# The feed-forward part behind the attention loop: batches taken by strip, products ahead in four banks, eight output buffers

## The reference, cut to what matters

```python
x = x + attn(cond(x, ...))
# low rank, ids choose A[i] (512 x 16) and B[i] (16 x 512) for each batch
y = (x @ B[i].T) @ A[i].T
# feed-forward part
h = layernorm(y) * gamma + beta
h = fake_quant(h) @ fake_quant(w1).T + b1      # a scale for each row: max|h| / 127
h = gelu(h)
h = fake_quant(h) @ fake_quant(w3).T + b3
out = x + h
```

## Time and profile before

| | |
|---|---|
| median of 3 runs | 602.52 us (602.12 to 605.37) |
| the profiled execution, its own time | 599.33 us |
| its span, first to last instruction | 597.5 us |
| busy over the span: PE, DVE, POOL, ACT | 95%, 83%, 67%, 55% |
| mean granted clock of PE | 0.99 of full |

### The profile page before, as it was taken

One profiled execution on the slowest core, in us unless ns is written; L12 is line 12 of the kernel. 1 busy time (PEld: TensorE's weight loads), 2 busy tenths in 40 slices (PEclk: granted clock), 3 DMA queues, 4 the chain that ended last, 5 costly groups with the idle time before them and its releaser, 6 DMA issues. The chain is left out here.

```text
span 597.5 us, 10369 instructions
## 1 busy us (share of the span) xinstructions
PE 568.8 (95%) x3107; PEld 430.4 (72%) x3107; DVE 495.5 (83%) x643; ACT 327.4 (55%) x877; POOL 401.0 (67%) x410
## 2 busy tenths in 40 slices
PE   6999979999999999999999999999999999987985
PEld 4545658888887788888878887888878888773342
DVE  2974558998999799979997999799979998867696
ACT  2142456556554655565556555655565555557594
POOL 3004288698679867976897689769966997751053
PEclk9999999999999999999999999999999999999699
DMA  9931334512451245124412442254123422100003
GB/s 277 250 70 35 82 95 125 128 49 57 133 127 47 58 128 132 42 60 135 123 45 60 131 114 53 55 146 103 51 66 107 105 47 59 36 1 0 1 2 142
DMA packets 38173, 51.93 MB, mean 87 GB/s; under 512 B 12101, under 2 KB 20453, under 8 KB 38149
## 3 DMA queue, kind: packets, MB, share of 16 engines
q1 hardware_dynamic: 35076, 45.89, 29.6%
q10 hardware_dynamic: 2592, 4.53, 2.3%
q0 software_dynamic: 480, 1.22, 0.6%
HBM read 28.55 MB, written 2.10 MB: 51 GB/s over the span
## 5 line engine op out<-in xcount | busy, mean ns | idle before, releaser
L1015 DVE SCALAR_TENSOR_TENSOR accT<-pair,so_now,accT 128x1024 f32<-128x1024 f32 x125 | 157.6, 1278 | 20.6 <-PE pair L1284 19.8
L1001 DVE SCALAR_TENSOR_TENSOR raw_q<-pair,sc_now,raw_q 128x1024 f32<-128x1024 f32 x90 | 115.5, 1283 | 3.5
L1283 PE MATMUL pair<-ctx_hi,wo 128*128 128x512 f32 x256 | 104.9, 410 | 2.6 <-issue 1.5
L677 ACT ACTIVATE probs<-flow,negmax 128x128 f32<-128x128 f32 x248 | 87.3, 369 | 34.3 <-DVE negmax L966 34.3
L1283 PE MATMUL pair<-h_hi,wq 128*128 128x512 f32 x240 | 100.9, 420 | 1.8 <-ACT raw_q L720 1.7
L1284 PE MATMUL pair<-ctx_lo,wo 128*128 128x512 f32 x256 | 100.4, 392 | 0.0
L1284 PE MATMUL pair<-h_lo,wq 128*128 128x512 f32 x240 | 94.4, 393 | 0.0
L528 POOL TENSOR_TENSOR probs<-probs,rowinv 128x512 f32<-128x512 f32 x64 | 66.7, 1042 | 28.3 <-DVE rowinv L988 28.3
L509 POOL TENSOR_TENSOR qT<-rope_c,rope_s 128x512 f32<-128x512 f32 x62 | 79.4, 1280 | 4.4
L497 POOL TENSOR_TENSOR rope_s<-swap_q,consts 128x512 f32<-128x512 f32 x62 | 80.3, 1295 | 2.1 <-DMA swap_q<-raw_q 2.1
L497 POOL TENSOR_TENSOR rope_c<-raw_q,consts 128x512 f32<-128x512 f32 x62 | 78.5, 1286 | 0.6
(11 more groups left out here) (229 smaller groups left out, 989.3 us busy)
## 6 DMA issues: line engine op xcount, KB each, us to landing
swap_q<-raw_q SPq DMA_DIRECT2D x62, 256.0 KB, 3.5
wq_i<-in_L_attn_qw_q SPq DMA_DIRECT2D x8, 1024.0 KB, 6.0
wo_i<-in_L_attn_qw_o SPq DMA_DIRECT2D x32, 256.0 KB, 2.7
swap_k<-raw_k SPq DMA_DIRECT2D x14, 256.0 KB, 3.6
wkv_i<-in_L_attn_qw_k SPq DMA_DIRECT2D x8, 256.0 KB, 3.8
wkv_i<-in_L_attn_qw_v SPq DMA_DIRECT2D x8, 256.0 KB, 4.0
out<-probsT SPq DMA_DIRECT2D x8, 256.0 KB, 2.0
stage<-in_x ACTq DMA_DIRECT2D x4, 256.0 KB, 4.6
```

The lines of the kernel that those rows point to most:

```text
L677: e = act.activation(probs[:, 0, f, seq(b)], bank[:, seq(b)], ACT.Exp, bias=negmax[:, f, b:b + 1], accum_out=rowsum[:, f, b:b + 1])
L1001: dve.scalar_tensor_tensor(out=into, in0=flat(pair[pair_of(h, (kind, j), last)][:, :, :]), scalar=sc_now[:, scale_slot(kind, h), j:j + 1], ...
L1015: dve.scalar_tensor_tensor(out=a, in0=flat(pair[pair_of(h, (O, c), last)][:, :, :]), scalar=so_now[:, (h if c == 0 else h - 1) % 2, c:c + ...
L1283: pe.matmul(into[:, f, :], w, upper[:, half[f]], start=True, stop=False)
```

## The change

1. The feed-forward part takes the batches in `LOW_ORDER`. "Batch b" there is now the b-th in this order; the number `LOW_ORDER[b]` is used where `low_h`, `rstd`, `accT` and `out` are addressed.
2. Four scaled products go out ahead, each as soon as the statistics of its bank are taken, in four banks (0, 2, 4, 6), one strip each. The other four go in two pairs of different strips (`scaled_pair`), a pair waiting once for `ln_done`.
3. The first two residuals are turned into banks 3 and 7, freed by ACT's squares, and bank 4 takes the others from the third on. The turned rows of the second layer use bank 3, those of its last batch bank 1.
4. Each of the eight batches has its own output buffer. The waits for landed DMAs go away.
5. The hand-written orders of PE, ACT, DVE and POOL are laid out anew. A few waits on buffers that the old order implied are now written out (`gelu_done` ahead of `scale_product(0, b)`, `ln_done` and `res_kept` ahead of the second layer's first products).

The numbers of each operation stay the same.

```diff
+        y_out = [t[:, f, :] for t in (probsT, swap_q, swap_k, probs[:, 1, :, :]) for f in range(2)]
...
-        SCALED, RESID = [banks[0], banks[2]], banks[4]
+        SCALED = [banks[0], banks[2], banks[4], banks[6], banks[0], banks[2], banks[0], banks[2]]
+        RESID = [banks[3], banks[7]] + [banks[4]] * (B - 2)
...
-                sp.dma_start(out[b, :, :], y_out[:, b % 2, :]).then_inc(d_out[b % 2], 16)
+                sp.dma_start(out[LOW_ORDER[b], :, :], y_out[b]).then_inc(d_out[b % 2], 16)
...
-                dve.scalar_tensor_tensor(out=y_ln[b], in0=SCALED[b % 2], scalar=rstd[:, 0, b:b + 1], in1=rows[:, 1, :],
+                dve.scalar_tensor_tensor(out=y_ln[b], in0=SCALED[b], scalar=rstd[:, 0, LOW_ORDER[b]:LOW_ORDER[b] + 1], in1=rows[:, 1, :],
...
+                if not m and b >= 2:
+                    dve.wait_ge(gelu_done, b - 1)
...
-                dve.wait_ge(d_out[b % 2], 16 * (b // 2))
-                dve.tensor_tensor(y_out[:, b % 2, :], probs[:, 0, b % 2, :], resid[b], ALU.add).then_inc(out_late, 1)
+                dve.tensor_tensor(y_out[b], probs[:, 0, b % 2, :], resid[b], ALU.add).then_inc(out_late, 1)
...
             norm(0)
+            norm(1)
             find_top(0, 0)
-            norm(1)
...
             def scaled_product(b):
-
-                if b == 0:
-                    pe.wait_ge(low_scaled, 1)
-                if b < 2:
-                    pe.wait_ge(stats_done, b + 1)
-                else:
-                    pe.wait_ge(ln_done, b - 1)
-                pe.matmul(SCALED[b % 2], low_h[STRIPS[b // 2], seq(b % 2)], low_gT[STRIPS[b // 2], :], start=True, stop=True).then_inc(scaled_done, 1)
+                seat = LOW_ORDER[b]
+                pe.matmul(SCALED[b], low_h[STRIPS[seat // 2], seq(seat % 2)], low_gT[STRIPS[seat // 2], :], start=True, stop=True).then_inc(scaled_done, 1)
+
+            def scaled_pair(p):
+                pe.wait_ge(ln_done, 4 * p - 6)
+                scaled_product(2 * p)
+                scaled_product(2 * p + 1)
...
-            scaled_product(0)
+            pe.wait_ge(low_scaled, 1)
+            for b in range(HB):
+                pe.wait_ge(stats_done, b + 1)
+                scaled_product(b)
             turn_residual(0)
-            scaled_product(1)
-            scaled_product(2)
             turn_residual(1)
...
```

More of the change, by code:

```diff
@@ L289, in two_seqs, with turned_rows @@
             return slice(2 * q * P, (2 * q + 2) * P)
-        SCALED, RESID = [banks[0], banks[2]], banks[4]
+        SCALED = [banks[0], banks[2], banks[4], banks[6], banks[0], banks[2], banks[0], banks[2]]
+        RESID = [banks[3], banks[7]] + [banks[4]] * (B - 2)
         LATE_OUT = 4
-        def turned_rows(m):
-            return banks[1 + 2 * m][:, 0:C * P // 2].bitcast(F16)
+        def turned_rows(m, b):
+            return banks[3 if m and b < B - 1 else 1][:, 0:C * P // 2].bitcast(F16)
         def layer_bank(m, b):
@@ L585, in _ @@
             add_bias(4)
+            add_residual(0)
             add_bias(5)
-            add_residual(0)
+            add_residual(1)
             add_bias(6)
-            add_residual(1)
             add_bias(7)
@@ L793, in keep_residual @@
                 act.wait_ge(resT_done, b + 1)
-                act.activation(resid[b], RESID, ACT.Copy).then_inc(res_kept, 1)
+                act.activation(resid[b], RESID[b], ACT.Copy).then_inc(res_kept, 1)
             def keep_yT(m, b):
                 act.wait_ge(yT_done[m], b + 1)
-                act.activation(y_qT[:, m, b % 2, :, :], turned_rows(m).rearrange("p (c n) -> p c n", c=C),
+                act.activation(y_qT[:, m, b % 2, :, :], turned_rows(m, b).rearrange("p (c n) -> p c n", c=C),
                                ACT.Copy, bias=-HALF_ZERO).then_inc(yT_kept[m], 1)
@@ L839, in _ @@
             keep_yT(1, 1)
+            round_rows(0, 7)
+            keep_yT(0, 6)
             round_rows(1, 2)
[L841 to L843 removed]
+            keep_yT(0, 7)
             gelu_rows(4)
             round_rows(1, 3)
[L846 removed]
             keep_yT(1, 2)
@@ L1142, in _ @@
             find_top(0, 5)
+            norm(6)
+            scale_product(0, 2)
             find_top(1, 0)
-            scale_product(0, 2)
+            norm(7)
+            scale_product(0, 3)
             find_top(1, 1)
-            norm(6)
-            scale_product(0, 3)
             find_top(0, 6)
-            find_top(1, 2)
-            norm(7)
             scale_product(0, 4)
             find_top(0, 7)
+            scale_product(1, 0)
+            find_top(1, 2)
+            scale_product(0, 5)
             find_top(1, 3)
-            scale_product(0, 5)
-            scale_product(1, 0)
+            scale_product(1, 1)
+            scale_product(0, 6)
             find_top(1, 4)
-            scale_product(0, 6)
-            scale_product(1, 1)
             find_top(1, 5)
             scale_product(0, 7)
-            find_top(1, 6)
             scale_product(1, 2)
             scale_product(1, 3)
+            find_top(1, 6)
             find_top(1, 7)
@@ L1504, in turn_residual @@
                     pe.wait_ge(b3_added, C)
-                    pe.wait_ge(stats_done, 3)
+                if b < 2:
+                    pe.wait_ge(squares_done, 2 * b + 2)
+                elif b == 2:
+                    pe.wait_ge(ln_done, 3)
                 else:
@@ L1508, in turn_residual @@
                 for c in range(C):
-                    mm = pe.transpose(RESID[:, seq(c)], accT[:, c, seq(b)], ident)
+                    mm = pe.transpose(RESID[b][:, seq(c)], accT[:, c, seq(LOW_ORDER[b])], ident)
                 mm.then_inc(resT_done, 1)
@@ L1515, in turn_rows @@
                 pe.wait_ge(rounded[m], b + 1)
-                if b >= 1:
+                if m == 1 and b == B - 1:
+                    pe.wait_ge(yT_kept[0], B)
+                elif b >= 1:
                     pe.wait_ge(yT_kept[m], b)
+                elif m == 1:
+                    pe.wait_ge(res_kept, 1)
                 for c in range(C):
-                    mm = pe.transpose(turned_rows(m)[:, seq(c)], rounded_rows(m, b)[:, seq(c)], ident_h[:, :])
+                    mm = pe.transpose(turned_rows(m, b)[:, seq(c)], rounded_rows(m, b)[:, seq(c)], ident_h[:, :])
                 mm.then_inc(yT_done[m], 1)
@@ L1525, in layer @@
                     pe.wait_ge(ff_scaled[0], b)
+                if m == 1 and b == 0:
+                    pe.wait_ge(ln_done, HB)
+                if m == 1 and b == 1:
+                    pe.wait_ge(res_kept, 2)
                 if m == 1 and b >= 2:
```

72 lines of the change are left out of this document (31 added, 41 removed).

## The result

| | before | with the change |
|---|---|---|
| median, us | 602.32 (4 runs, 600.44 to 605.37) | 594.02 (4 runs, 592.96 to 594.74) |
| ratio, with its 95% interval | | 0.9856 (0.9811 to 0.9901) |
| the profiled execution: time, span | 599.33, 597.5 | 592.96, 591.1 |
| its mean granted clock | 0.990 | 0.993 |
| first `norm` to the end of the last residual | 41.95 | 36.44 |

The kernel is 8.3 us faster. I had forecast 3.7 us, and no more than 5.7 us within the range (602.52 to 596.8). The change was timed a second time on another chip, in six runs against seventeen of before: 594.66 us (593.48 to 596.79) against 601.39 (598.17 to 603.63), ratio 0.990 (0.9869 to 0.9932), so 6.7 us. Both are more than forecast.

The account below looks back on a forecast made before the run. DVE was taken to bound the tail, with PE the bound at the low clock. Terms of 1.6 and 2.5 us made 4.1, taken as 3.7: 602.52 to 598.8 us, range 596.8 to 602.4.

Parts of the forecast that it names:

- The bound: Tail from the first `norm`: DVE carries the most work, idle 8.2 us, the most any order can give.
- The pair, the products ahead, the buffers: Tail: four products ahead cost the path nothing, a low-clock pair takes 2.0 us, eight buffers remove 1.9 us of DMA waits.
- Term two: From `scale_product(0, 1)` to the last residual: DVE waits fall from 3.4 to 0.9 us, 2.5 us gained.
- Term one: From the first `norm` to `scale_product(0, 1)`: that product starts at 565.6 instead of 567.21, 1.6 us earlier.
- I leave the low clock from 554.54 to 564.8: Start of the tail: the half-clock stretch stays where it was, since PE's wait ahead of it stays.
- The first rival: Tail: clock returns with the first layer, 2.3 us earlier, gaining 0.7 to 1.2 us more (597.6 to 598.1 us); chance 0.2.
- The sum for the profiled execution: Whole tail: 4.1 us from both terms, taken as 3.7 us walk against walk; span 597.5 to 593.8 us.
- I carry the difference over unchanged: Whole run: the profiled execution's 3.2 us below the median stays as an offset, giving 602.52 - 3.7 = 598.8 us.
- The rival that ends slower: Behind PE's wait: more transposes keep the clock low past 564.8; 600.4 to 605.8 us; chance 0.15, a third past 580.
- The last sentence of the prediction: Tail: if the span shrinks over 3 us but the median doesn't, the clock is the first suspect.

Follow-up runs that it names:

- after_again: The changed kernel run once more, unaltered, on another chip: median 594.66 us, ratio to before 0.990; tail 36.76 us in its trace.
- before_filled: Kernel before, with two extra full-height matmuls, their result unread, in PE's wait for the first `norm`: median 596.24 us, ratio to before 0.9932.
- before_eight_buffers: Kernel before, with eight output buffers in place of two, all else as before: median 600.84 us, ratio to before 0.9993.
- after_natural_strips: Changed kernel with batches taken in the order 0 to 7, so both products of a pair share a strip: median 595.63 us, ratio to before 0.9922.
- after_two_buffers: Changed kernel with two output buffers and the waits for landed DMAs put back: median 595.15 us, ratio to before 0.9903.
- the 45 runs: Runs of the unchanged kernel before, beside the experiments on three chips: 598.1 to 604.9 us at mean clocks of 0.977 to 0.990.
- its three fillers: Changed kernel with unread work in PE's wait: two full-height matmuls (594.01 and 593.31 us), two 32-row matmuls (594.34 us), or sixteen transposes (593.13 us).
- before_full_height: Kernel before, with scaled products over all 128 partitions instead of the strip's 32, giving another output: median 595.04 us, ratio to before 0.9897.
- after_full_height: Changed kernel, no filler, with scaled products over all 128 partitions instead of a strip, giving another output: median 593.67 us, ratio to before 0.9866.

## Why the prediction was wrong, step by step

**The bound.** Right. DVE carried the tail, PE ahead of it, and no order could give more than the 8.2 us of DVE's idle time. The changed tail took 36.44 us and, with the clock kept, 34.65 us, against a floor of 33.7.

**The pair, the products ahead, the buffers.** Right in mechanism. One reading beside it was wrong: the prediction has 4.7 products at the low level before, and the earlier trace rows show two whole ones and parts of two, 2.8 in all; the sum doesn't use this number. The pair goes at one price, 1.13 us at the full level and 2.08 at the low one; I had taken 2.0. No wait for a product or a DMA is left, and the waits for the first two `scale_product` are 0.49 and 1.10 us, where I had 1.2 and 1.9.

**Term two, what comes behind `scale_product(0, 1)`.** Right: 2.5 us forecast. From its start to the end of the last residual the trace of before has 595.01 - 567.21 = 27.8 us, that of the change 588.64 - 563.44 = 25.2: 2.6 us. Whether all of the 1.9 us of DMA waits count in it is not shown: alone, the buffers gave half a microsecond, within the noise.

**Term one, the start of the chain.** Too small: 1.6 us forecast, 14.15 - 11.24 = 2.9 us measured from the first `norm` (2.6 in `after_again`). The step that failed is "I leave the low clock from 554.54 to 564.8". Counted from the first `norm`, the clock came back after 11.7 us before, and after 9.6 and 9.1 us in the two traces of the change, 2.1 to 2.6 us earlier. Of the 1.3 us missed, 0.5 lie ahead of the end of `layer(0, 0)` (7.7 us after the first `norm` against 8.2 forecast; there the pair had met the full clock) and 0.8 between it and `scale_product(0, 1)` (3.5 against 4.3), where the clock came back.

The first rival had "a return 2.3 us earlier", with a chance of 0.2. Its number came true, but its rule, a return with the first layer, doesn't hold in the other traces. In that of `before_filled` the first layer ends at 560.92 and the clock comes back at 567.2, 6.3 us later; in that of `before_eight_buffers` it ends at 562.62 and the clock comes back at 567.5, 4.9 us later; in that of `after_natural_strips` the clock is back 0.3 us ahead of its end. The rows of the first layer in the first two:

```profile
559.01 1.91 PE L1529 MATMUL pair<-ffT,y_qT 128*128 128x512 bf16 x4
```

```profile
560.71 1.91 PE L1527 MATMUL pair<-ffT,y_qT 128*128 128x512 bf16 x4
```

So the rival was right by luck. What the traces do show is that the return came 9.1 to 9.6 us behind the first `norm` in four traces of the changed order (`after`, `after_again`, `after_two_buffers`, `after_natural_strips`), and 11.7 to 15.3 us behind it in three of the old one (`before`, `before_filled`, `before_eight_buffers`). Why is open.

**The sum for the profiled execution.** 3.7 us forecast and 5.5 measured in the tail. Of the 1.8 us missed, 1.3 are term one and 0.1 term two. The other 0.4 are what the prediction took off when it went from 4.1 to 3.7, on the ground that small waits escape the walk after as before; the two terms by themselves were not too large. Of the profiled execution's time, 6.4 us went (599.33 to 592.96): 0.9 us of that is the earlier start of the tail, which isn't the change's doing.

**"I carry the difference over unchanged."** This is the step that failed most. I saw that the profiled execution was 3.2 us below the median and that one trace doesn't say where that lies. By the line through the 45 runs, 3.2 us are 8.9 us of low clock more. That all of it lies in the tail is likely but not shown, since no run of before with so much has a trace, and three of the other traces have 3.4 us of it in the loop. The chain of numbers for the second comparison, with all runs and their clocks: at the changed kernel's own low time, 10.1 us, before would take 594.9 + 0.358 x 10.1 = 598.5 us (10.1 is below the 12 to 28 us that the line rests on), and the change takes 594.66. That is 3.9 us of gain at equal clock. The other 0.358 x (17.7 - 10.1) = 2.7 us are low time that the change spares, and 3.9 + 2.7 = 6.6 of the 6.7 measured. In the first comparison the change had only 5.6 us of low time and before, if its median of 602.32 lies on the line, some 20.7: there 2.9 us are the gain at equal clock and 5.4 the clock's.

That 3.9 is near my 3.7 is luck, since the gain at equal clock depends on the clock at which it is taken. A line through the 32 runs of the changed order with all its products in strips (the change and its three fillers) is 593.3 us + 0.15 x low time (correlation 0.45), less than half as steep as that of before. Between the two lines lie 1.6 us at no low time and 0.2 us more for each us of it, which points the same way as the tails above (1.4 to 2.0 us at none, 5.2 us at 10.2). The last sentence of the prediction, that the clock would be the first suspect, pointed there; it should have been a term of the sum.

**The rival that ends slower.** It feared that the stretch behind the wait, with more transposes in it, would keep the clock low for longer. It didn't: the stretch was 6.8 us in one trace of the change and 10.2 in the other, and 10.2 before. What I took for poor cover, the transposes, kept most of the clock as filler, and what I took for solid work, the scaled products, was what lost it.

**What stays open.** Which of the strip-high products matter, those ahead of PE's wait or those behind it, isn't told apart: `before_full_height` changes all of them. In the changed kernel eight plain products of the same height stay ahead in every version, the clock is kept in `after_full_height` all the same, and so those alone don't do it. Nor is it known why the same program has 12 us of low clock in one run and 28 in another. That `before_eight_buffers` gained only 0.55 us in the median at the same low time isn't explained either. Last, the start of the first `norm` moves a single execution by up to 4.4 us, and it isn't independent of the clock: it starts at 554.30 to 556.56 in the four traces with no low clock in the tail, and at 552.20 to 553.50 in seven of the eight with 6.8 us or more (555.29 in `after_two_buffers`). Which of them follows the other, if either, isn't known. That is why the case for the height of the products rests on the clocks of all runs and not on the trace of `before_full_height` alone.

## What to carry to other kernels

Compare the profiled execution with the median before any sum is made, and ask each run's mean granted clock where the difference lies: if it is in the stretch that is changed, it is a term of the sum and not an offset. A matmul that uses a quarter of the array's rows takes as long as a full one and can cost the clock of what follows. Put such products side by side for their own time (2.08 us instead of 3.77 at the low level); for the clock, what helped here was fuller work in and around PE's wait. Whether rows filled with zeros would do was not tried. Keep what others wait for out of the low stretch: the same 10.2 us at half clock cost one order 5.3 us and the other 1.6 to 2.1. Waits that are removed alone can bring less than their rows say: in the trace of `before_eight_buffers` 1.6 of 1.9 us came back as other waits.

## What the runs showed of the hardware

- The same products in the same order with 128 rows instead of 32 took 1.12 us each (1.09 before), and the mean clock went from 0.985 (17 runs) to 0.9965 (4 runs), the median from 601.33 to 595.04 us.
- A gap of 2.29 us in PE's work left the clock at full level (`before_full_height`), and in `after_again` it fell at 552.4 while PE had no gap at all from 551 to 553.
- Filling PE's wait was not enough in the old order: in the trace of `before_filled` PE was idle for 0.19 us at the wait, and the clock fell at 556.96 for 10.2 us; five of its eight runs kept clocks of 0.995 to 0.998.
- One program on one chip ran at mean clocks from 0.977 to 0.990, and over 45 runs each microsecond at the low level went with 0.36 us of time; in the changed order it was 0.15 us over 32 runs.
- Products of two strips went side by side at either level: 1.13 and 2.08 us for a pair, against 3.77 us for two of one strip at the low one.
